# First edges of visits in a graph network kernel: 19 plain transfers, a row load and a turn by TensorE in place of 21 gathers

## What is computed

```
edge_index = jnp.stack([src, dst])
h = jnp.maximum(_layernorm(x, axis=-1), 0.0)
x = x + gnn0(h, edge_index)      # two graph convolutions: out[dst] += (h @ W)[src] * dinv[src] * dinv[dst]; then + b
h = jnp.maximum(_layernorm(x, axis=-1), 0.0)
x = x + gnn1(h, edge_index, edge_attr_32)
#   msg  = relu(concat(h[src], edge_attr) @ W1 + b1);  agg = segment mean of msg over dst
#   out  = relu(concat(h, agg) @ W2 + b2)
return x
```

## Time and profile before

| | us |
|---|---|
| median of 3 runs | 2456.9 (2456.45 to 2467.43) |
| the profiled execution | 2462.0 |
| its span | 2460.1 |
| PE busy | 2155.0 (88%) |
| DVE busy | 1870.1 (76%) |
| POOL busy | 1822.6 (74%) |
| ACT busy | 1241.6 (50%) |

### The profile page before, as it was taken

The page is one execution under the profiler, slowest core; times in us unless marked ns, Lnnn a source line. Parts: engine busy times, 40 slices in busy tenths (PEclk is TensorE's granted clock), DMA queues, the critical chain, the costliest instruction groups (busy, mean ns, idle before and its releaser), DMA issues.

```text
span 2460.1 us, 45677 instructions
## 1 busy us (share of the span) xinstructions
PE 2155.0 (88%) x15568; PEld 1771.9 (72%) x15569; DVE 1870.1 (76%) x3574; ACT 1241.6 (50%) x3349; POOL 1822.6 (74%) x1687
## 2 busy tenths in 40 slices
PE   0344899999999998799995599999999999999996
PEld 0133679997667897688884487887787878888885
DVE  6999999998889884544447377777777777777777
ACT  5846246665666773555557243444444434444440
POOL 0867877888888787777777777777777777777770
PEclk9867999999999998999998799999999999999999
DMA  9414233333334351588874243434434343434432
GB/s 359 173 39 140 74 127 127 135 126 126 124 124 163 141 188 45 166 325 302 322 282 149 70 145 103 142 109 121 131 106 145 106 141 109 131 120 118 133 86 60
DMA packets 127247, 358.89 MB, mean 146 GB/s; under 512 B 34082, under 2 KB 77831, under 8 KB 117687
## 3 DMA queue, kind: packets, MB, share of 16 engines
q10 hardware_dynamic: 24752, 186.56, 19.9%
q0 software_dynamic: 56880, 85.25, 13.5%
q1 hardware_dynamic: 45369, 84.00, 9.9%
HBM read 229.75 MB, written 125.93 MB: 145 GB/s over the span
## 4 chain that ended last, share of the span: by engine, by line
PE 52%; POOL 17%; DVE 15%; issue 8%; ACT 4%; DMA 3%; DVEq 1%; POOLq 0%; ACTq 0%; SPq 0%
POOL rows L803 14%; PE ps_feat L1102 6%; PE ps_node L1102 6%; PE ps_node L1117 5%; PE ps_feat L1117 5%; DVE region_c L2079 5%; PE ps_sum L1212 3%; ACT rows L1318 3%; PE pre_banks L1090 3%; PE ps_extra L1250 3%; POOL permuted L821 2%; PE pre_banks L1203 2%; PE ps_feat L1234 2%; PE ps_node L1234 2%; PE ps_sum L1234 2%
## 5 line engine op out<-in xcount | busy, mean ns | idle before, releaser
L821 POOL DMA_INDIRECT permuted<-rows_or_lows,slot_of_edge x768 | 902.5, 1175 | 234.0 <-issue 151.7
L803 POOL DMA_INDIRECT rows<-table,region_a x800 | 786.1, 983 | 243.8 <-issue 236.8
L2079 DVE TENSOR_TENSOR region_c<-iota_key,region_c 128x1568 bf16<-128x1568 f16 (+1 forms) x327 | 355.8, 1088 | 0.0
L1435 ACT ACTIVATE region_a<-pre_banks 128x392 bf16<-128x392 f32 x392 | 195.0, 499 | 146.3 <-PE pre_banks L1090 138.3
L1102 PE MATMUL ps_node<-region_a,region_b 128*128 128x256 bf16 (+1 forms) x1911 | 263.8, 268 | 4.1 <-issue 4.1
L1102 PE MATMUL ps_feat<-region_a,region_b 128*128 128x256 bf16 x1764 | 252.5, 272 | 0.0
L584 DVE CAST wide_counts<-region_a 128x1024 fp32r<-128x1024 bf16 (+2 forms) x163 | 117.2, 723 | 156.4 <-PE ps_node L1117 69.1
L1250 PE MATMUL ps_extra<-msg_parts,target_hot 128*128 128x256 f32 x1176 | 222.7, 305 | 13.8 <-DVE msg_parts L2264 13.6
L582 ACT ACTIVATE wide_counts<-region_a 128x1024 fp32r<-128x1024 bf16 x150 | 158.6, 1060 | 120.7 <-PE ps_node L1117 56.9
L2279 DVE TENSOR_TENSOR target_hot<-consts,region_a 128x512 fp32r<-128x512 f32 x336 | 207.5, 618 | 1.0
L1212 PE MATMUL ps_sum<-onehot,rows 128*128 128x64 f32 x1600 | 202.3, 270 | 0.0
(11 more groups left out here) (319 smaller groups left out, 4790.0 us busy)
## 6 DMA issues: line engine op xcount, KB each, us to landing
counts<-region_a ACTq DMA_DIRECT2D x23, 3136.0 KB
region_a<-counts ACTq DMA_DIRECT2D x11, 3200.0 KB
region_a<-counts ACTq DMA_DIRECT2D x11, 3072.0 KB
rows_or_lows<-block_lows ACTq DMA_DIRECT2D x72, 448.0 KB
permuted<-region_b SPq DMA_DIRECT2D x25, 833.0 KB, 24.4
region_a<-permuted SPq DMA_DIRECT2D x24, 833.0 KB
rows_or_lows<-edge_cols_in POOLq DMA_DIRECT2D x24, 544.0 KB
region_a<-attr_t_in SPq DMA_DIRECT2D x50, 256.0 KB, 2.8
```

Source lines behind the costliest of these rows:

```text
L803: nc.gpsimd.indirect_dma_start(rows[:, s, j * D:(j + 1) * D], None, tables[2], bass.IndirectOffsetOnAxis(ap=message_rows[:, c * TC + j:c * ...
L821: nc.gpsimd.indirect_dma_start(permuted, bass.IndirectOffsetOnAxis(ap=slot_of_edge[:, r * RT + k:r * RT + k + 1], axis=0), edge_rows_of[:, ...
L1435: nc.scalar.activation(counts[strip % 2][:, :, j * W:j * W + W], count_banks[w % BANKS][:, 0:KEYS].rearrange("p (d h) -> p h d", h=SB), AC ...
L2079: v.tensor_tensor(hot_key(u)[:, :, 0:n], iota_key[:, None, 0:n].to_broadcast([P, UNIT // SIDE, n, SIDE]), keys[:, :, None, :].to_broadcast ...
```

## The change

The 21 gathers of first edges leave POOL. A new table in device memory, `visit_starts_dram` ("starts_of_visits"), gets one entry for each visit. It is filled from the table of first edges by 19 plain transfers from device memory to device memory, ten issued by SP and nine by ACT. Each serves a run of targets that lie a fixed step apart and get the same number of visits k: the source repeats each entry k times (a step of 0), so each element is 4 bytes. When all 19 have landed SP loads the table as 21 rows of 128 (`visit_starts_i`), DVE shifts and converts it, PE turns it, and DVE adds the places and stores `visit_row`. This stands ahead of node phase 0 on DVE and PE. The plan of places shrinks from two integer tables to one. `find_visits` is gone.

```diff
+def runs_of(parts):
+
+    runs, visit = [], 0
+    for target, k in parts:
+        if runs and runs[-1][3] == k and (runs[-1][2] == 1 or target - runs[-1][1] == runs[-1][2] * runs[-1][4]):
+            first, at, n, _, step = runs[-1]
+            runs[-1] = (first, at, n + 1, k, step if n > 1 else target - at)
+        else:
+            runs.append((visit, target, 1, k, W))
+        visit += k
+    return runs
...
+START_RUNS = runs_of(VISIT_TARGETS + [(0, VB * P - sum(VISITS))])
...
+        def spread_starts(engine, run):
+
+            visit, target, n, k, step = run
+            of = starts_dram[target:target + n * step].rearrange("(n w) a -> n w a", w=step)[:, 0:1].to_broadcast([n, k, 1])
+            engine.dma_start(visit_starts_dram[visit:visit + n * k].rearrange("(n k) a -> n k a", k=k), of,
+                             allow_slow_non_contiguous=True).then_inc(starts_gathered, 16)
...
@@ block.sync, after the load of ends_i
+            sp.wait_ge(starts_moved, 16)
+            for run in START_RUNS[0::2]:
+                spread_starts(sp, run)
+            sp.wait_ge(starts_gathered, 16 * len(START_RUNS))
+            sp.dma_start(visit_starts_i, visit_starts_dram.rearrange("(b p) a -> b (p a)", p=P)).then_inc(starts_gathered, 16)
...
@@ block.gpsimd
-            pool.wait_ge(starts_moved, 16)
-            for b in range(VB):
-                nc.gpsimd.indirect_dma_start(
-                    visit_start[:, b:b + 1], None, starts_dram,
-                    bass.IndirectOffsetOnAxis(ap=visit_plan[:, 0, b:b + 1], axis=0)).then_inc(starts_gathered, 16)
-            pool.wait_ge(visit_rows_ready, 1)
+            pool.wait_ge(visit_rows_ready, 3)
...
@@ block.tensor, ahead of the node phases
+            pe.wait_ge(visit_rows_ready, 1)
+            nc.tensor.transpose(ps_sum[0][:, 0:VB], visit_starts, ident[0:VB, 0:VB]).then_inc(visit_rows_ready, 1)
...
@@ block.scalar, after the search, before root
+            act.wait_ge(starts_moved, 16)
+            for run in START_RUNS[1::2]:
+                spread_starts(act, run)
...
@@ block.vector
             ranks_taken(EARLY - 1)
+            dve.wait_ge(starts_gathered, 16 * len(START_RUNS) + 16)
+            link(v.tensor_single_scalar(visit_starts_i, visit_starts_i, 4, ALU.arith_shift_right))
+            v.tensor_copy(visit_starts, visit_starts_i).then_inc(visit_rows_ready, 1)
             with dve.If(mixed < 1):
                 dve.wait_ge(starts_turned, 2)
                 v.tensor_copy(count[:, 0:SB], ps_sum[1][:, 0:SB])
                 dve.drain()
+            dve.wait_ge(visit_rows_ready, 2)
+            v.tensor_tensor(visit_row[:], ps_sum[0][:, 0:VB], visit_plan[:], ALU.add).then_inc(visit_rows_ready, 1)
...
-            def find_visits():
-
-                dve.wait_ge(starts_gathered, 16 * VB)
-                link(v.tensor_single_scalar(visit_start[:], visit_start[:], 4, ALU.arith_shift_right))
-                v.tensor_tensor(visit_row[:], visit_start[:], visit_plan[:, 1], ALU.add).then_inc(visit_rows_ready, 1)
...
-                        if n == 0 and g == VISIT_ROWS_AT:
-                            find_visits()
```

More of the change, by code:

```diff
@@ L116 @@
 BUILT_BEFORE = [max((v + 1 for v in range(u) if KEY_PARTS[v] & KEY_PARTS[u] or v % HOT_UNITS == u % HOT_UNITS), default=0) for u in range(UNITS)]
+VISIT_TARGETS = [(w * W + j * (W // len(splits)), k) for w, splits in zip(WINDOW_AT, SPLITS) for j, k in enumerate(splits)]
+def runs_of(parts):
[8 more added lines that the diff above has]
+    return runs
 VB = (sum(VISITS) + P - 1) // P
+START_RUNS = runs_of(VISIT_TARGETS + [(0, VB * P - sum(VISITS))])
 VISIT_PARTS = [range(0, 13), range(13, VB)]
@@ L157, in build @@
         tiles_dram = nc.dram_tensor("tiles", (2, NT), I32, kind="Internal").ap()
+        visit_starts_dram = nc.dram_tensor("starts_of_visits", (VB * P, 1), I32, kind="Internal").ap()
         starts_dram = nc.dram_tensor("starts_of_nodes", (NP, 1), I32, kind="Internal").ap()
@@ L240, in build @@
         visit_key_kept = carve(VB)
+        visit_starts_i = carve(P, I32)[0:VB]
+        visit_starts = carve(P)[0:VB]
         used[0] = 0
@@ L296, in build @@
         messages_of = region_c[:, 0:NB * D].rearrange("p (b d) -> p b d", d=D)
-        visit_plan = sb("visit_plan", [P, 2, VB], I32)
-        visit_start = sb("visit_start", [P, VB], I32)
+        visit_plan = sb("visit_plan", [P, VB], I32)
         visit_row = sb("visit_row", [P, VB], I32)
@@ L2370 @@
     at = ROW * np.arange(EDGE_ROWS)[:, None] + np.arange(P)[None, :]
-    visit_of = np.zeros((3, VB * P), np.int32)
-    parts_of = [(w * W + j * (W // len(splits)), k) for w, splits in zip(WINDOW_AT, SPLITS) for j, k in enumerate(splits)]
-    target_of = np.concatenate([np.full(k, target) for target, k in parts_of])
-    visit_of[0, :sum(VISITS)] = target_of
-    visit_of[1, :sum(VISITS)] = np.concatenate([np.arange(k) for _, k in parts_of]) * (P // ROW)
-    visit_of[2, :sum(VISITS)] = -target_of * SB
-    visit_of = visit_of.reshape(3, VB, P).transpose(2, 0, 1)
+    visit_of = np.zeros((2, VB * P), np.int32)
+    visit_of[0, :sum(VISITS)] = np.concatenate([np.arange(k) for _, k in VISIT_TARGETS]) * (P // ROW)
+    visit_of[1, :sum(VISITS)] = -SB * np.concatenate([np.full(k, target) for target, k in VISIT_TARGETS])
+    visit_of = visit_of.reshape(2, VB, P).transpose(2, 0, 1)
     node_half = P * np.arange(SB)[None, :] + np.arange(P)[:, None] - 0.5
@@ L2382 @@
                                 RANGES * RANGE_ROWS + np.arange(P * RT).reshape(P, RT), np.tile(np.arange(KEYS), (P, 1)),
-                                np.triu(np.ones((P, P)), 1), visit_of[:, 2], node_half, -node_half], 1).astype(np.float32)
+                                np.triu(np.ones((P, P)), 1), visit_of[:, 1], node_half, -node_half], 1).astype(np.float32)
     arrays = {
@@ L2390 @@
         "consts": constants,
-        "visit_plan": visit_of[:, :2],
+        "visit_plan": visit_of[:, 0],
         "edge_cols": np.concatenate([attr.view(np.int32), src[:, None], dst[:, None]], 1)[:DT * P].reshape(DT, P, ROW_WORDS).transpose(1, 0, 2),
```

1 line of the change is left out of this document (removed).

## The result

The median of five runs is 2471.3 us (2468.38 to 2471.94); five runs of the kernel before, among them those shown above, have a median of 2459.4. The ratio is 1.0044, 95% interval 1.0024 to 1.0064: the changed kernel is slower, by 12 us, and by less than the 0.5% that the chances used as a bound. The prediction was 2443.1 with a range up to 2468; the result lies above the range. Its rival (2), a stall that outweighs the gain, is what came; it had a chance of 0.18.

The account below looks back on a forecast made before the run. It took the message stage to start with the later of POOL's unbroken queue and table 2; a start 13.8 us earlier gave 2462.0 - 13.8 = 2448.2 us, or 2443.1 for the median, which lay 5.1 lower; range 2440 to 2468.

Parts of the forecast that it names:

- rival (2): Ahead of node phase 0: transfers above 33 ns an element stall DVE beyond the gain; at 56 ns 2476.6 us; chance 0.18.
- What bounds the kernel: Message stage: 1029.6 us, starts with the later of POOL's arrival and table 2 at 1355.4, shifts as a whole.
- What the change takes from POOL: POOL's queue: starts 20.1 us earlier, is through its scatters 15.6 us earlier, at 1355.5; no pacing wait.
- What it adds to the main chain: DVE and PE ahead of and in node phase 0: +1.8 us, range +0.8 to +5; message start 1357.3, 13.8 earlier.
- rival (3): Node phase 0: PE's slow clock stays through the first groups, main chain +5, gain 10.6, 2446.3 us; chance 0.13.
- Are the transfers there in time?: Before DVE's shift: 19 transfers landed by 162.4 us, 3.7 to spare, with 847 elements on the busiest engine.
- the price of an element: Transfers into the new table: 12 ns for each 4-byte element, from above 56 ns; limit 16.4 ns.
- The issues cost nothing: SP and ACT before node phase 0: both idle, 0.31 us an issue, ten done by 152.
- The sum: Whole kernel: 2462.0 - 13.8 = 2448.2 us against the profiled execution, 2443.1 for the median.

Follow-up runs that it names:

- e6: Changed kernel with seven long runs laid out by ACT as rows in SBUF and copied in 14 transfers; 2447.56 us, ratio 0.9948 to the kernel before.
- e5: Changed kernel with all long transfers cut as in e1 and one table entry in every 64 bytes; 2450.22 us, one run.
- e2: Changed kernel with DVE's shift and cast, PE's turn and DVE's add moved behind groups 7 and 8 of node phase 0; 2485.9 us, ratio 1.0104 to the kernel before.
- e4: Changed kernel with the same 19 transfers in opposite order, long ones first; 2468.64 us, one run.
- e3: Changed kernel with one transfer cut, that of 191 targets into 176 and 15; 2463.26 us, one run.
- e1: Changed kernel with all long transfers cut into a multiple of 16 targets and a rest, 27 transfers; 2455.6 us, ratio 0.9974 to the kernel before.
- e8: Changed kernel, its 19 transfers uncut, with one table entry in every 64 bytes; 2454.28 us, ratio 0.9967 to the kernel before.
- e9: e5 with one table entry in every 32 bytes instead of 64; 2453.95 us, one run.

## Why the prediction was wrong

- **What bounds the kernel: right.** The message stage starts with the later of POOL and table 2, and moves as a whole. Every kernel of the table bears it out, with 1.4 us between the landing of table 2 and POOL's start where the prediction had 0.1.
- **What the change takes from POOL: right for e6, but the rule for it needs a second term.** A lead of 20.5 us (167.05 for 187.57) became 15.0 at the last scatter (1354.80 for 1369.83); predicted were 20.1 and 15.6. No pacing wait stood in the way, in any kernel. Where node phase 0 is late as well, POOL's lead shrinks much more (the table below the list).
- **What it adds to the main chain: right at its start, and at its end by some luck.** In e6 the first `rows_of` is at 168.70 (predicted 169.0), the message gather at 1357.01 (1357.3). But table 2 was there at 1355.6, 1.6 us before the 1357.2 of the prediction, and POOL started 1.3 us later behind it than predicted. PE's granted clock was 0.50 up to 172 us, where the kernel before had 0.99 from 168 on, and 1.00 from 174 on; the second `rows_of` still followed after 3.1 us, so rival (3) didn't come.
- **"Are the transfers there in time?": the step that failed**, by one term of its sum, the price of an element. I took 12 ns, for the busy time of a packet of 4 bytes, and 1.4 us for everything fixed. Measured in the same formula: (39.1 - 1.4) / 847 = 44.5 ns. Of the 39.1 us, 32.2 are up to the last packet and 6.9 behind it. The stall then is 0.847 x 44.5 - 13.9 = 23.8, and 1.2 more because the load took 3.5 us (187.47 to 190.97) and not 2.3: 25.0, against 25.05 seen. Rival (2) is what happened, and the price lies between the two ends, 12 and 56.
- **Why 12 was the wrong end.** The row was misread: its 640 packets are not elements. In the raw records each gather of 128 entries leaves 32 packets, 16 of 32 bytes (8 entries) that took 15 ns and 16 of 4 bytes that took 9; 12 is their mean, and 640 packets of 4 bytes would not have made the 0.01 MB of the row. But the right reading, a few ns, would have been further off still: most 4-byte packets of the transfers did take about 9 ns (table under e5). What the row could not show is what happens when they write 4 bytes beside 4 bytes in device memory; the gathers wrote to SBUF. Spacing the writes took 22.8 us off (39.1 to 16.3), cutting the transfers 15.1, both together 26.0. So the number of elements on one engine isn't the whole cause, and its 44.5 ns are no constant: 17.6 or less with the writes apart, and in the dense table the steps from 847 to 489 to 201 elements give (39.1 - 29.8) / 358 = 26 and (29.8 - 24.0) / 288 = 20 ns.
- **"The issues cost nothing": wrong, though hidden here.** 0.31 us was the issue of a store of 52 rows; here the ten took 17.2 us and the nine 25.9. In the changed kernel DVE's wait covered it, in e2 it cost 10 us.
- **The sum.** With the stall the prediction's own start would be 1357.3 + 25.05 = 1382.4; seen were 1384.4. In medians, 2459.4 - 13.8 + 25.05 = 2470.7; measured 2471.3.

How late or early (-) each kernel is against the kernel before, in us:

| kernel | first `rows_of` | POOL's first gather of visits | POOL's last scatter | the last by the rule below |
|---|---|---|---|---|
| changed | 26.0 | 4.7 | 11.3 | 9.5 |
| e4 | 22.4 | 1.1 | 6.4 | 5.9 |
| e3 | 15.9 | -5.4 | 1.9 | -0.6 |
| e1 | 9.2 | -12.1 | -5.1 | -7.3 |
| e8 | 4.8 | -16.5 | -7.7 | -11.7 |
| e9 | 4.2 | -17.1 | -7.7 | -12.4 |
| e5 | 1.5 | -19.8 | -14.1 | -15.0 |
| e6 | 0.8 | -20.5 | -15.0 | -15.8 |

What POOL is ahead counts against the stages of the other engines, since an instruction of POOL takes 1.62 us beside node phase 0 and 1.26 before the messages, and those stages move when node phase 0 moves. So the rule is: the last scatter moves by as much as `rows_of`, less 15.6 / 20.1 of what POOL gained on it. In the changed kernel that is 26.0 - 0.776 x 21.3 = 9.5 us. It gives the direction everywhere but in e3 and is off by 0.5 to 4.7 us, most in e8 and e9. It was found after the runs and not tested. The trace shows where the changed kernel loses most: scatters 337 to 432, near 767 to 924 us, took 156.8 us for 147.8 before.

What stays open: how the memory or the engines make neighbouring writes wait (a rewrite of a larger piece, or an order kept among writes to it); these runs show only that it goes with the distance, between 4 and 64 bytes. Also open is the rest of POOL's lateness behind that rule. In the changed kernel it cost nothing, since table 2 came later still; in e1, e8 and e9 it set the start. The main chain has a spread of its own: from the first `rows_of` to the last store of table 2 it took 1183.5 us in the kernel before, 1183.3 in e6 and 1175.7 in e5, and no run tells why.

## What to carry to other kernels

Here a transfer of single 4-byte elements from memory to memory was priced by where its writes lay, not by the packets of a gather: measure one of its own kind before putting it ahead of a stage. What helped in these runs was to make the elements long (rows laid out in SBUF), to keep small writes 64 bytes apart, and to give each transfer a number of entries that 16 divides. Before taking a price from a row of packets, check packets times size against the bytes beside it. Where the price is open, place the wait where something else is late anyway, and look at what stands behind it on each queue, the issuing engine's own work included. A saving on one queue is worth what the next in line allows: in e6 14.1 of 20.5 us (1357.01 for 1371.09), and only if nothing new is put on the other chain.

## What the runs showed of the hardware

- 2688 writes of 4 bytes side by side in device memory, from 19 transfers, needed 39.1 us; the same with 64 bytes between them 16.3. With all transfers cut, 24.0, 15.4 and 13.1 us at 4, 32 and 64 bytes.
- The last transfer counted as landed 6.9 us after the last recorded packet's end in the changed kernel and 7.5 in e1; with 64 bytes between the writes 1.7 (e8) and 0.5 (e5).
- A packet of 4 bytes took 9 ns or less for half of them, and up to 2.4 us for some, in the changed kernel; none took over 9 ns in e5.
- Issuing stalls: the nine transfers took ACT 25.9 us, one single issue 19.4 of them, behind transfers of 348 and 382 elements; in e2 `root` came only after the last issue, at 176.29. Cut, 13 issues took it 9.9 us (e5).
